# Gated cross-attention: the last 128 rows computed with rows on the output partitions, the other 672 in parts of 416 and 256

## What is computed

```python
memory_proj    = ctx @ W_mem.T                          # (8, 722, 1024)
scores         = x @ memory_proj^T / sqrt(1024)         # (8, 100, 722)
memory_context = softmax(scores) @ memory_proj          # (8, 100, 1024), "mc" in the kernel
gate  = sigmoid(concat(x, memory_context) @ W_gate.T + b_gate)
fused = x + gate * memory_context
out   = fused * rsqrt(mean(fused**2, -1) + 1e-6) * norm_w
```

## Time and profile before

| | |
|---|---|
| median of 3 runs | 295.5 us |
| profiled execution, its own time | 295.5 us |
| its span, first to last instruction | 293.7 us |
| granted TensorE clock, mean | 0.996 |
| TensorE busy | 288.1 us (98%), 1623 matmuls |
| DVE busy | 171.1 us (58%) |
| ACT busy | 160.7 us (55%) |
| POOL busy | 4.5 us (2%) |
| bytes moved | 49.56 MB, mean 169 GB/s |

### The profile page before, as it was taken

How to read it: one execution, slowest core, us unless ns; L and a number is a source line. 1 busy time by engine, 2 the same in 40 slices (tenths; PEclk the granted TensorE clock), 3 DMA queues, 4 the chain that set the end, 5 groups by cost and what they waited for, 6 DMA issues and landing times.

```text
span 293.7 us, 4047 instructions
## 1 busy us (share of the span) xinstructions
PE 288.1 (98%) x1623; PEld 268.4 (91%) x1623; DVE 171.1 (58%) x239; ACT 160.7 (55%) x237; POOL 4.5 (2%) x11
## 2 busy tenths in 40 slices
PE   8999999999999999999999999999999999999993
PEld 8999999898998989899898999999988888889992
DVE  2667554558566585865758563334436855238594
ACT  5548344555484635649354445534543865356574
POOL 2000000000000000000000000000000000001002
PEclk9999999999999999999999999999999999999998
DMA  6999370792938759295783310268203410000256
GB/s 205 400 376 307 125 296 0 195 332 83 327 123 241 282 136 352 51 331 186 199 321 116 102 43 35 71 235 358 70 20 127 143 71 3 0 0 2 50 208 227
DMA packets 21363, 49.56 MB, mean 169 GB/s; under 512 B 2864, under 2 KB 3760, under 8 KB 21344
## 3 DMA queue, kind: packets, MB, share of 16 engines
q1 hardware_dynamic: 21344, 49.30, 50.3%
HBM read 45.75 MB, written 3.28 MB: 167 GB/s over the span
## 4 chain that ended last, share of the span: by engine, by line
PE 97%; issue 0%; ACT 0%; DVE 0%; POOLq 0%; POOL 0%; ACTq 0%
PE ps L343 70%; PE ps L437 11%; PE ps L460 9%; PE ps L451 1%; PE ps L464 1%; PE ps L357 1%; PE ps L471 1%; PE ps L368 0%; PE ps L378 0%; PE ps L374 0%; PE ps L371 0%; PE ps L383 0%; PE ps L380 0%; PE ps L537 0%; POOLq L57 0%
## 5 line engine op out<-in xcount | busy, mean ns | idle before, releaser
L343 PE MATMUL ps<-act_hi,w_hi 128*128 128x400 f32 (+2 forms) x264 | 78.0, 347 | 0.0
L343 PE MATMUL ps<-act_lo,w_hi 128*128 128x400 f32 (+2 forms) x264 | 77.4, 344 | 0.0
L343 PE MATMUL ps<-act_hi,w_lo 128*128 128x400 f32 (+2 forms) x264 | 77.3, 344 | 0.0
L343 PEld LDWEIGHTS ps<-act_hi,w_hi 128*128 128x128 f32 x264 | 48.4, 188 | 2.9
L343 PEld LDWEIGHTS ps<-act_lo,w_hi 128*128 128x128 f32 x264 | 49.0, 188 | 1.8
L343 PEld LDWEIGHTS ps<-act_hi,w_lo 128*128 128x128 f32 x264 | 49.1, 188 | 1.8
L809 DVE TENSOR_TENSOR w_lo<-w_stage,w_hi 128x1024 fp32r<-128x1024 f32 (+2 forms) x23 | 26.0, 1132 | 23.9 <-ACT w_hi L590 22.7
L809 DVE TENSOR_TENSOR cn_lo<-cn_stage,cn_hi 128x1536 fp32r<-128x1536 f32 (+1 forms) x16 | 23.8, 1485 | 5.7 <-ACT cn_hi L609 5.6
L809 DVE TENSOR_TENSOR ct_lo<-ct_stage,ct_hi 128x1444 fp32r<-128x1444 f32 x16 | 25.8, 1653 | 0.5 <-ACT ct_hi L601 0.5
L590 ACT ACTIVATE w_hi<-w_stage 128x1024 fp32r<-128x1024 f32 x20 | 21.0, 1054 | 6.9 <-PE ps L343 5.1
L677 ACT ACTIVATE pc<-ps,row_inv 100x512 f32<-100x512 f32 x8 | 5.5, 688 | 31.6 <-PE ps L464 31.6
(11 more groups left out here) (124 smaller groups left out, 464.7 us busy)
## 6 DMA issues: line engine op xcount, KB each, us to landing
ct_stage<-ctxT SPq DMA_DIRECT2D x16, 722.0 KB, 7.8
cn_stage<-ctxN SPq DMA_DIRECT2D x8, 768.0 KB, 5.9
cn_stage<-ctxN SPq DMA_DIRECT2D x8, 512.0 KB, 4.2
w_stage<-w_gate_x SPq DMA_DIRECT2D x8, 512.0 KB, 5.9
w_stage<-w_gate_mc SPq DMA_DIRECT2D x8, 512.0 KB, 3.5
x_again<-xT SPq DMA_DIRECT2D x1, 3200.0 KB, 11.3
cn_stage<-ctxN SPq DMA_DIRECT2D x8, 320.0 KB
acc<-xT SPq DMA_DIRECT2D x6, 400.0 KB, 7.8
```

What stands on the lines that cost most here:

```text
L343: done = nc.tensor.matmul(o, wgt, stream[h][part], start=first and wgt is wh and part == 0, stop=last and wgt is wl, skip_group_check=onto)
```

## The change

- FIRST becomes 416 and a new ROWS = 672. The transposed steps cover 672 rows in parts of 416 and 256 columns: still 16 of them (NT = 16). Their results leave transposed, all 672 rows.
- The last 128 rows get three steps of their own (`gate_rows`), for feature tiles 0 to 2, 3 to 5 and 6 to 7: now the parts of memory_context are stationary (128 features x 128 rows) and the gate weights stream, 384, 384 and 256 columns, so that the result has rows on the partitions. Each is 24 matmuls. For this the split gate weights of a group lie side by side (`w_groups`).
- What these steps need by rows: memory_context and the x half of the gate, with the bias added by one DVE instruction (`add_bias`), are transposed by 16 TensorE transposes behind step 11 (`turn_last_rows`) into PSUM banks 0 to 3 and read from there. x and the norm weight come by rows from memory (`x_last`, 512 KB, and `norm_row`, broadcast to 128 partitions), into `w_stage` after the last weight split.
- The last rows' squares are summed along the free dimension by ACT in the same instruction as the squaring (`accum_out`), so their mean needs no TensorE; POOL makes the root, and the root scales by partition.
- The mean of the second part (256 columns) is made by TensorE inside the first row step (`means_second`), its root by POOL, and two transposes inside the second row step (`turn_roots`) put the root in all partitions; DVE multiplies with it in `output_second`.
- The turns of the other rows, the three chunks of the last step and the packed 32 rows are gone. The last rows are stored in two halves of 512 features.

```diff
-FIRST, SMALL = 512, 32
-CHUNKS = ((FIRST, FIRST + P), (FIRST + P, FIRST + 2 * P), (R - SMALL, R))
+FIRST, ROWS = 416, R - P
+SLICES = ((FIRST, FIRST + P), (FIRST + P, ROWS))
+GROUPS = ((0, 3), (3, 6), (6, 8))
...
+STEPS = [(0, 0, FIRST), (1, 0, FIRST), (0, FIRST, ROWS)] + [(t, 0, FIRST) for t in range(2, KD)] \
+    + [(t, FIRST, ROWS) for t in range(1, KD)]
+NT = len(STEPS)
+LAST = NT + len(GROUPS) - 1
...
@@ sync
+            sp.wait_ge(w_lo_done, J_G2 + KD)
+            sp.dma_start(fused_rows, x_last).then_inc(rows_in, 16)
+            sp.dma_start(norm_rows, norm_row.partition_broadcast(P)).then_inc(rows_in, 16)
             sp.wait_ge(rooted, 1)
...
+            for k in range(0, KD, 2):
+                sp.wait_ge(out_done, KD + k + 2)
+                sp.dma_start(out_v[:, k:k + 2, FIRST:ROWS], acc[:, k:k + 2, FIRST:ROWS]).then_inc(stored, 16)
+            for i in range(2):
+                half = slice(i * D // 2, (i + 1) * D // 2)
+                sp.wait_ge(row_left, i + 1)
+                sp.wait_ge(row_right, i + 1)
+                sp.dma_start(out_rows[:, half], row_out[:, half]).then_inc(stored, 16)
@@ tensor
+            def turn_last_rows():
+                pe.wait_ge(mc_saved, KD)
+                for t in range(KD):
+                    done = nc.tensor.transpose(turned_tile(MC_ROWS, t), mc[:, t, ROWS:R], ident[:, :])
+                done.then_inc(mc_turned, 1)
+                pe.wait_ge(biased, 1)
+                for t in range(KD):
+                    done = nc.tensor.transpose(turned_tile(GX_ROWS, t), acc[:, t, ROWS:R], ident[:, :])
+                done.then_inc(gx_turned, 1)
+            def gate_rows(n, after=None, work=None):
+                pe.wait_ge(seeded, n - 1)
+                for k in range(KD):
+                    xh, xl = act_hi[:, k, ROWS:R], act_lo[:, k, ROWS:R]
+                    wh, wl = (a[:, :, k * P:(k + 1) * P] for a in w_groups[n - NT])
+                    for act_part, w_part in ((xh, wh), (xh, wl), (xl, wh)):
+                        done = nc.tensor.matmul(gate_bank(n).rearrange("p (t c) -> p t c", c=P), act_part, w_part,
+                                                start=False, stop=k == KD - 1 and act_part is xl,
+                                                skip_group_check=True)
+                    if k == after:
+                        work()
+                done.then_inc(gate_made, 1)
+            def means_second():
+                for i, (a, b) in enumerate(SLICES):
+                    pe.wait_ge(summed, NT - 1)
+                    nc.tensor.matmul(late_mean(i), square_sum[:, a:b], mean_w[:, :], start=True, stop=False)
+                    pe.wait_ge(squared, NT)
+                    done = nc.tensor.matmul(late_mean(i), square[:, (NT - 1) % 2, a - FIRST:b - FIRST], mean_w[:, :],
+                                            start=False, stop=True)
+                done.then_inc(late_mean_made, 1)
+            def turn_roots():
+                pe.wait_ge(late_rooted, 1)
+                for i in range(len(SLICES)):
+                    done = nc.tensor.transpose(bank(RMS, P, P, i * P), rms_late[:, i:i + 1].to_broadcast([P, P]),
+                                               ident[:, :])
+                done.then_inc(rms_turned, 1)
...
-            for n in range(END0 + 3, LAST + 1):
+            for n in range(END0 + 3, NT):
                 gate_mc(n)
-            turn(0, 0, KD - 1)
...
+                if n == END0 + 3:
+                    turn_last_rows()
+            gate_rows(NT, 4, means_second)
+            gate_rows(NT + 1, 1, turn_roots)
+            gate_rows(NT + 2)
@@ scalar, last row steps: sigmoid without a bias, then
+                    nc.scalar.activation(square[:, n % 2, 0:cols.stop - cols.start], fused_rows[:, cols], ACT.Square,
+                                         scale=float(D) ** -0.5,
+                                         accum_out=last_mean[:, n - NT:n - NT + 1]).then_inc(squared, 1)
...
+            finish(LAST)
+            for i in range(2):
+                left = slice(i * D // 2, i * D // 2 + D // 4)
+                if i == 0:
+                    act.wait_ge(last_rooted, 1)
+                act.wait_ge(rows_weighted, i + 2)
+                nc.scalar.activation(row_out[:, left], row_out[:, left], ACT.Copy,
+                                     scale=rms_last[:, :]).then_inc(row_left, 1)
@@ vector
-                if n == END0 + 3:
+                if n == END0 + 4:
                     dve.wait_ge(weighted, END0 + 1)
                     dve.wait_ge(rms_in, 16)
-                while done < min(KD, 2 * (n - END0 - 2)):
+                while done < min(KD - 2, 2 * (n - END0 - 3)):
                     output(done)
                     done += 1
...
+            output(KD - 2)
+            output(KD - 1)
+            dve.wait_ge(late_mean_made, 1)
+            nc.vector.tensor_scalar(rms_late[:, :], bank(MEANS, 2, P, 2 * Q), EPS, None, ALU.add)\
+                .then_inc(mean_copied, 1)
+            dve.wait_ge(mc_turned, 1)
+            dve.wait_ge(rows_in, 32)
+            rows_times(NT)
+            rows_fuse(NT)
+            dve.wait_ge(weighted, NT)
+            dve.wait_ge(rms_turned, 1)
+            for k in range(5):
+                output_second(k)
+            rows_times(NT + 1)
+            rows_fuse(NT + 1)
+            for k in range(5, KD):
+                output_second(k)
+            rows_weigh(NT)
+            dve.wait_ge(squared, NT + 2)
+            nc.vector.tensor_scalar(early_mean[:, :], last_mean[:, 0:1], last_mean[:, 1:2], EPS, ALU.add, ALU.add)\
+                .then_inc(early_mean_set, 1)
+            rows_times(LAST)
+            rows_fuse(LAST)
+            rows_weigh(NT + 1)
+            dve.wait_ge(squared, LAST + 1)
+            dve.wait_ge(early_mean_set, 1)
+            nc.vector.tensor_tensor(rms_last[:, :], last_mean[:, 2:3], early_mean[:, :], ALU.add)\
+                .then_inc(mean_copied, 1)
+            rows_weigh(LAST)
```

More of the change, by code:

```diff
@@ L72, in build @@
         w_stage = sb(top, "w_stage", [P, 2, WB])
-        w_hi = [sb(top, f"w_hi{i}", [P, WB], F32R) for i in range(2)]
-        w_lo = [sb(top, f"w_lo{i}", [P, WB], F32R) for i in range(2)]
+        w_turn = [sb(top, f"w_turn_{part}", [P, 2 * WB], F32R) for part in ("hi", "lo")]
         ident = sb(top, "ident", [P, P])
@@ L98, in build @@
         mc = sb(top, "mc", [P, KD, R])
[L99 to L102, removed]
+        x_again = sb(top, "x_again", [P, KD, ROWS])
+        gate = sb(top, "gate", [P, 2, FIRST])
+        square = sb(top, "square", [P, 2, FIRST])
+        square_sum = sb(top, "square_sum", [P, ROWS])
         mean_w = sb(top, "mean_w", [P, 1])
@@ L316, in _ @@
                 sp.wait_ge(out_done, k + 2)
[L317 to L333, removed]
+                sp.dma_start(out_v[:, k:k + 2, 0:FIRST], acc[:, k:k + 2, 0:FIRST]).then_inc(stored, 16)
+            for k in range(0, KD, 2):
[6 more added lines that the diff above has]
+                sp.dma_start(out_rows[:, half], row_out[:, half]).then_inc(stored, 16)
+            sp.wait_ge(stored, 16 * (KD + 2))
         @block.tensor
@@ L533, in mean_of_last @@
-            def mean_of_last(i):
-                a, b = CHUNKS[i]
-                pe.wait_ge(squared, LAST + 1 + i)
-                nc.tensor.matmul(late_mean(i), square[:, LAST % 2, a - FIRST:b - FIRST] if i < NC - 1
-                                 else small_sum[:, 1, :], mean_w[:, :], start=False, stop=True)\
-                    .then_inc(late_mean_made, 1)
-            def turn(i, t0, t1):
-                a, b = CHUNKS[i]
-                for t in range(t0, t1):
-                    side, at = (t // 2 % 2, t % 2 + t // 4 * 2) if i == 0 else (t // 4, t % 4)
-                    done = nc.tensor.transpose(bank(TURN[i][side], P, P, at * P), acc[:, t, a:b], ident[:, :])
-                return done
@@ L549, in turn_small @@
-            def turn_small():
-                for j in range(2):
-                    done = nc.tensor.transpose(bank(TURN[NC - 1][j], P), small[:, j, :], ident[:, :])
-                return done
+            def turn_last_rows():
[7 more added lines that the diff above has]
+                done.then_inc(gx_turned, 1)
@@ L726, in sigmoid @@
             def sigmoid(n):
+                act.wait_ge(gate_made, n + 1)
+                if n >= 2:
+                    act.wait_ge(fused, n - 1)
+                if n >= NT:
+                    w = (GROUPS[n - NT][1] - GROUPS[n - NT][0]) * P
+                    nc.scalar.activation(gate[:, n % 2, 0:w], gate_bank(n), ACT.Sigmoid).then_inc(gate_done, 1)
+                    return
                 t, r0, r1 = STEPS[n]
@@ L760, in _ @@
             act.wait_ge(gx_saved, 2 * B)
[L761 removed]
+            for n in range(LAST + 1):
                 if n in SPLIT_AT:
                     split_gate_w(SPLIT_AT[n])
[L764 removed]
+                early = n == END0 + 1 or n >= NT
                 if early:
@@ L996, in _ @@
```

(10 more changed lines are left out.)

243 lines of the change are left out of this document (105 added, 138 removed).

## The result

The changed kernel took 296.83 us (median of 4 runs, 296.54 to 297.03), the kernel before 295.52 beside it: ratio 1.0042, 95% interval 1.003 to 1.0055. The forecast was 296.9, in a range of 295.2 to 298.6. The profiled execution took 296.5 us with a span of 294.8; the span of before was 293.7, so 1.1 us of the 1.3 show in this pair of traces.

What follows compares the result with a forecast made beforehand. TensorE's stream to the last gate matmul plus the tail bound the kernel. Stream +0.45+1.94+0.80 = +3.2 us, tail -1.8, sum +1.4: span 295.1, time 296.9 us, with 8 in 10 for 295.2 to 298.6.

Steps and rivals of the forecast that it cites:

- Small instructions in front of F: TensorE before the last gate matmul: 18 transposes and 8 mean instructions paid in full, 1.94 + 0.80 us.
- F: End of the last gate matmul on TensorE: 285.39 us before, forecast 288.6; the tail follows it.
- (a): Rival: the small instructions vanish in TensorE's stream beside the long matmuls; 294.1 us, faster; chance 0.10.
- (b): Rival: no difference, small instructions half hidden at about 55 ns, or last store landing in about 1.4; 295.6 us; chance 0.12.
- Gate matmuls: TensorE's gate stage: same columns but 72 more matmuls, each at a fixed cost, +0.45 us.
- the fixed 6.3 ns: Cost of each gate matmul apart from its columns, from the line through 512 and 288 columns.
- No waits in front of F: TensorE before the last gate matmul: weights, bias, means and roots arrive in time; priced at nothing.
- about even: First mean: its sum and TensorE both come earlier by similar amounts; if late, a wait of 0.1 or 0.2 us.
- Tail -1.8: From the last gate matmul to the span's end: 6.5 us where it was 8.3, last store issued 3.7 after.
- Rival (d): DVE or the first mean is late: +0.5 to 1.0 us, 297.6 us; chance 0.10, within the forecast's 0.70.
- Clock: Rival: transposes do not count as activity, so TensorE's clock could drop to 1.2 GHz: 298.4 us; chance 1 in 50.

Runs made afterwards that it cites:

- the last experiment: The changed kernel with row steps of 3, 2 and 3 feature tiles, so the last is 384 columns wide and not 256: 297.22 us, ratio 1.0056.

## Why the prediction held, step by step

- **Small instructions in front of F: right, in full.** Forecast 1.94 + 0.80 = 2.74. Measured 1.73 for the 16 transposes (4.58-2.85), 0.87 for the second mean and 0.22 for the two roots (row steps of 5.07 and 4.42, against 24 matmuls of 384 columns that start 175 ns apart, 4.20), 2.82 in all. Doubling the transposes, taking 12 away and placing 16 in the kernel before each gave the same 108 to 109 ns. Rivals (a) and (b) are refuted by that; the other way to (b), a last store that lands in 1.4 us, did not come either (2.2).
- **Gate matmuls: the size too large, the sign not shown.** +0.45 was forecast. The stream moved by 2.88, of which 2.82 are the above and some 0.17 the first mean, so -0.1 is left. The mis-sized term is the fixed 6.3 ns, taken from a line through 288 and 512 columns: 416 columns measured 4.54 us (189.0 ns, not 189.8), 256 columns 118.8 (not 119.2), and each extra matmul cost 4.6 ns where only that was changed. Added up by these step lengths the gate stage would be 0.1 longer; the kernel before lost that in its first two steps, which took 5.62 us each for 5.57 (they start at 214.65 and 220.27, the third at 225.90), for a reason that was not looked into.
- **No waits in front of F: right but for the first mean.** Its sum was 0.07 us late and it cost 0.17 more than before, where the prediction had called it "about even" and allowed 0.1 or 0.2. The second mean and the roots follow the matmuls ahead of them without idle time; the squares of the second mean were ready 0.27 us before TensorE asked (278.11, 278.38), half of the 0.5 forecast. DVE's wait for the broadcast root, 2.0 us before, is gone, as forecast.
- **Tail -1.8: right as a sum, with terms off both ways.** Issue of the last store F+3.7 forecast, F+3.8 measured: the sum of squares is read by an instruction of its own (0.19 us) that the forecast did not have, and the root took 0.67, not 0.54, while the sigmoid took 0.38, not 0.47; from the issue to the end of the span it was 0.1 less than before (256 KB landed in 2.2, not 2.4). DVE's backlog and the last sigmoid ended within 0.03 us of each other (288.70, 288.67), and the product started at 288.71, so this trace alone does not say which held it; the last experiment, in which DVE was idle, does. Rival (d) is out but for the 0.17 of the first mean.
- **Clock: no drop**, behind 1.7 us or 3.5 us of transposes.
- **The time, 296.9 against 296.83, is closer than its terms, and that part is luck.** The stream was put 0.3 too high (+3.2 for +2.88): the gate matmuls 0.5 too high, the small instructions 0.1 and the first mean 0.17 too low. Span against span the change is +1.1, not the forecast +1.4; the medians differ by 1.3.
- The forecast and the rivals were told apart by one question, whether small instructions hide under long matmuls, and the trace of before had already answered it in two places.

The kernel before needed its transposes too, but after F, where they overlapped with ACT, DVE and POOL working on the last chunks. The change shortened the tail by 1.8 us and paid 2.9 us for it on the engine that has no idle time up to F.

## What to carry to other kernels

Work moved from the tail into the stream of the bound engine costs its full price there; count it instruction by instruction before counting what the tail gains. If it must be early, give it to engines with idle time: here DVE and the DMA queues turned the same rows at no cost that the time shows, once the queue's issues were few enough not to stand in front of a store that others wait for. A DMA on a shared issuing engine costs its issue time, and what is queued behind it pays. And a wait that reaches the bound engine can cost more than its length: here 9.2 us of standing brought 2.7 us at the lower clock.

## What the runs showed that I had not expected

- Sixteen stores of 32 KB in pieces of 128 bytes took 10.4 us to issue (0.65 each); eight stores of 64 KB in pieces of 512 bytes 3.74 us (0.47 each).
- DVE turned 1024 columns (eight runs of 128) in 32 x 32 blocks in 1.24 us; I had put 2.2, from 1.12 for 512 columns read with a stride.
- An activation that sums along the free dimension is followed by an instruction of 0.19 us that reads the sum.
- In the pause of 9.2 us TensorE's granted clock fell to 0.50. It stayed there over the first 12 matmuls of 384 columns, 320 ns apart, and was back at 1.00 from 291.1 us on, where they start 175 ns apart again.
